# Moving VectorE's sums of x, its scaling, and the convolution kernel's products within the last pair of head groups

## The reference

```
base  = x @ W.T                                    # W 512 x 512
low   = x @ lora_A[label of b]                     # 5 labels, 512 x 32 each
x     = x + base + (low @ lora_B.T) * 0.5
K     = 2 * Re(sum_n Ct[h,n] * exp(dtA[h,n] * t))  # a kernel of 512 taps for each head
y     = causal convolution of x with K per head + x * D
x     = x + y * (position < length of b)
```

## Time and profile before

| quantity | value |
| --- | --- |
| median of 3 runs | 191.71 us (191.71 to 192.05) |
| profiled execution | 192.15 us |
| its span, first to last instruction | 190.4 us |
| TensorE busy | 185.3 us, 97% |
| VectorE busy | 141.7 us, 74% |
| ScalarE busy | 94.4 us, 50% |
| GpSimd busy | 68.1 us, 36% |

### The profile page before, as it was taken

The page is one execution under the profiler, slowest core; times in us unless marked ns, Lnnn a source line. Parts: engine busy times, 40 slices in busy tenths (PEclk is TensorE's granted clock), DMA queues, the critical chain, the costliest instruction groups (busy, mean ns, idle before and its releaser), DMA issues.

```text
span 190.4 us, 2677 instructions
## 1 busy us (share of the span) xinstructions
PE 185.3 (97%) x920; PEld 155.3 (82%) x920; DVE 141.7 (74%) x193; ACT 94.4 (50%) x149; POOL 68.1 (36%) x111
## 2 busy tenths in 40 slices
PE   7999999999999999999899999999999999999994
PEld 3487887888887888887688878889999999999994
DVE  0579979977998968778997865467777777777743
ACT  2447066098183972331663571606565656565600
POOL 6000878000000058810001034315676767676700
PEclk9999999999999999999999999999999999999999
DMA  6697997000000000000000155015887888888534
GB/s 176 155 380 281 427 422 332 4 2 0 3 2 0 0 2 0 3 0 0 0 0 9 36 193 160 5 55 121 288 284 275 281 274 276 278 284 273 190 120 156
DMA packets 14813, 27.35 MB, mean 144 GB/s; under 512 B 2608, under 2 KB 5072, under 8 KB 13904
## 3 DMA queue, kind: packets, MB, share of 16 engines
q1 hardware_dynamic: 14128, 26.66, 40.9%
q10 hardware_dynamic: 672, 0.52, 1.0%
HBM read 18.71 MB, written 8.47 MB: 143 GB/s over the span
## 4 chain that ended last, share of the span: by engine, by line
PE 77%; DVE 9%; POOL 6%; ACT 4%; issue 3%; DVEq 0%; POOLq 0%
PE k_ps L810 13%; PE k_ps L792 6%; POOL tmp L420 5%; PE k_ps L793 5%; PE k_ps L794 5%; PE y_ps L725 5%; PE y_ps L726 5%; PE y_ps L727 5%; DVE low_sel L1043 5%; PE k_ps L811 3%; PE y_ps L741 3%; DVE phase L1063 2%; PE y_ps L745 2%; PE y_ps L732 2%; PE low_ps L719 2%
## 5 line engine op out<-in xcount | busy, mean ns | idle before, releaser
L502 POOL TENSOR_TENSOR t_lo<-w_raw,t_hi 128x512 fp32r<-128x512 f32 x32 | 40.9, 1284 | 38.4 <-ACT t_hi L571 38.4
L1115 DVE COPY_PREDICATED x_all<-len_mask,k_ps 128x512 f32<-128x512 int32 x31 | 23.4, 753 | 16.0 <-PE k_ps L794 16.0
L565 ACT CAST xs_hi<-x_all 128x512 fp32r<-128x512 f32 x32 | 19.9, 623 | 26.0 <-PE k_ps L794 26.0
L725 PE MATMUL y_ps<-x_hi,w_hi 128*128 128x512 f32 x72 | 28.2, 392 | 0.0
L726 PE MATMUL y_ps<-x_hi,w_lo 128*128 128x512 f32 x72 | 28.1, 390 | 0.0
L727 PE MATMUL y_ps<-x_lo,w_hi 128*128 128x512 f32 x72 | 28.1, 390 | 0.0
L1043 DVE COPY_PREDICATED low_sel<-lab_mask,low_ps 32x512 f32<-32x512 int32 x32 | 23.4, 731 | 3.4 <-PE low_ps L855 1.1
L792 PE MATMUL k_ps<-xs_hi,t_hi 128*128 128x384 f32 (+1 forms) x68 | 22.3, 327 | 0.0
L1055 DVE TENSOR_TENSOR xs_lo<-x_all,xs_hi 128x512 fp32r<-128x512 f32 x32 | 22.0, 692 | 0.0
L793 PE MATMUL k_ps<-xs_hi,t_lo 128*128 128x384 f32 (+1 forms) x68 | 20.8, 306 | 0.0
L794 PE MATMUL k_ps<-xs_lo,t_hi 128*128 128x384 f32 (+1 forms) x68 | 20.8, 305 | 0.0
(11 more groups left out here) (216 smaller groups left out, 403.6 us busy)
## 6 DMA issues: line engine op xcount, KB each, us to landing
w_raw<-k_pad SPq DMA_DIRECT2D x32, 256.0 KB, 4.2
out<-x_all SPq DMA_DIRECT2D x31, 256.0 KB, 3.4
x_all<-in_xt SPq DMA_DIRECT2D x7, 1024.0 KB, 12.0
w_raw<-in_wt SPq DMA_DIRECT2D x3, 256.0 KB, 4.5
x_all<-in_xt SPq DMA_DIRECT2D x3, 256.0 KB, 4.7
a_raw<-in_a_lab SPq DMA_DIRECT2D x1, 320.0 KB, 5.5
w_raw<-in_wt ACTq DMA_DIRECT2D x1, 256.0 KB, 3.2
x_all<-in_xt ACTq DMA_DIRECT2D x1, 256.0 KB, 4.3
```

Of the source, the lines that this page charges most:

```text
L502: g.tensor_tensor(t_lo[:, k % TR, :], t_raw[:, k % RAW, ::-1], f32(t_hi[:, k % TR, :]), ALU.subtract).then_inc(t_lo_done, 1)
L565: s.copy(xs_hi[:, h % XR, :], x_all[:, h, :]).then_inc(xs_hi_done, 1)
L725: mm(o, w_hi[:, c, cols(d)], moving(x_hi, g, c), start=(c == 0), stop=False, skip_group_check=True)
L1115: v.copy_predicated(x_all[:, h, :], mask, y2_ps[h % 2]).then_inc(o_done, 1)
```

## The change

VectorE makes all four sums of x, and the low parts of T3 and T2, in group 4's step; `k_scale` moves from group 4's step behind group 5's selection, where it stands ahead of `k_factors_lo`. ScalarE casts T2 ahead of `stack_low(5)` instead of behind it, and `copy_k` moves from between `evict(5, 2)` and `evict(5, 3)` to behind `stack_low(6)`. TensorE does `k_matmuls` behind the pair's products of A instead of ahead of group 5's last `times_b`, and M6 ahead of M1, which keeps the wait for `k_copied`. Branches that `PAIRS = (6,)` never takes are removed.

```diff
-        m_order = ("M1", "M6", "M5", "M7", "M2", "M3", "M4")
+        m_order = ("M6", "M1", "M5", "M7", "M2", "M3", "M4")
...
                 if g == FIRST - 1:
                     split_op_hi(0, "T3")
+                    split_op_hi(0, "T2")
                 if g != 1:
                     stack_low(g)
-                if g == FIRST - 1:
-                    split_op_hi(0, "T2")
...
                     split_op_hi(0, "T4")
                     split_op_hi(0, "T1")
-                    copy_k()
                 evict(g, 3)
...
                 stack_low(g)
+                copy_k()
...
-                if g == PE_KGEN:
-                    k_matmuls()
                 times_b(g, 3)
...
                 low_of(g + 1, False, True, a_hi[:, 0:2, :], a_lo[:, 0:2, :], i, "T3").then_inc(low_done, 1)
-                if g == PE_KGEN + 1:
-                    pe.wait_ge(k_copied, 1)
...
-                for d in range(2):
-                    product(alpha, d, w11_hi, w11_lo, i, "X11", True).then_inc(m_done, 1)
+                k_matmuls()
                 wait_op(i, "T2")
...
                     product(beta, d, s_high[1], s_low[1], i, "T2", True).then_inc(m_done, 1)
+                pe.wait_ge(k_copied, 1)
+                for d in range(2):
+                    product(alpha, d, w11_hi, w11_lo, i, "X11", True).then_inc(m_done, 1)
...
                 if g == DVE_KGEN + 1:
-                    sum_x(0, "T1")
-                    sum_x(0, "T3")
-                    k_scale()
-                if g == FIRST - 1:
-                    sum_x(0, "T2")
-                    sum_x(0, "T4")
+                    for name in sum_order:
+                        sum_x(0, name)
                     split_op_lo(0, "T3")
                     split_op_lo(0, "T2")
+                if g == FIRST - 1:
+                    k_scale()
                     k_factors_lo()
                     length_mask()
```

More of the change, by code:

```diff
@@ L652, in _ @@
                     s.copy(s_high[3], s_raw[3]).then_inc(s_hi_done, 1)
-                if g == PE_KGEN + 1 and i > 0:
-                    copy_k()
                 stack_low(g)
+                copy_k()
                 act.wait_ge(op_lo_done, lo_at(i, "T4"))
@@ L662, in _ @@
                 stack_low(g + 1)
[L663 to L676, removed]
+                for h in range(LEAD):
+                    split_t_hi(h)
+                    if h < 2:
+                        split_xs_hi(h)
                 act.wait_ge(op_lo_done, lo_at(i, "T1"))
@@ L681, in _ @@
                         .then_inc(alpha_read, 1)
-                if i + 1 < len(PAIRS):
-                    split_op_hi(i + 1, "T2")
             for h in range(2, LEAD):
@@ L953, in _ @@
                 pair(i)
-                if PAIRS[i] == PE_KGEN - 1:
-                    pe.wait_ge(alpha_read, 4 * i + 4)
-                    k_matmuls()
             for h in range(LAST):
@@ L1209, in _ @@
                     mix(d, x_all[:, b, cols(d)], x_all[:, a, cols(2 + d)], beta, "M6")
-                if g == PE_KGEN - 1:
-                    k_scale()
                 for d in range(2):
@@ L1217, in _ @@
                     mix(d, u3, u3, gamma, "M5")
[L1218 to L1225, removed]
+                for h in range(2):
+                    split_xs_lo(h)
                 for d in range(2):
@@ L1231, in _ @@
                     mix(d, m1, m1, beta, "M4")
-                if i + 1 < len(PAIRS):
-                    split_op_lo(i + 1, "T2")
             for h in range(2, LEAD):
```

## The result

The changed kernel took 193.23 us (median of 7 runs, 192.31 to 193.37) against 192.05 for the kernel before in the same comparison: ratio 1.0047, 95% interval 1.003 to 1.0064, so 0.6 to 1.2 us slower. The forecast was a shift of +0.91. One launch of the kernel before took 299.04 us, far from its other six (191.71 to 192.47); no trace shows why.

What follows compares the result with a forecast made beforehand. TensorE, busy 97% of the span, was taken to bound the kernel through its waits; 0.18 from VectorE's chain and 0.73 from ScalarE's copies, +0.91 on 191.71, gave 192.6 us, range 192.3 to 193.1 (8-in-10: 191.9 to 193.3).

Steps and rivals of the forecast that it cites:

- The wait for T3's cast: VectorE before group 5's selection: T3's low part waits for ScalarE's cast, so the selection starts only 0.34 us earlier.
- the sum: Shift of group 7's `plus_b`, +0.91 us, put on the median 191.71 to give 192.6 us.
- the forecast's own range: Range of the main forecast without rivals: 192.3 to 193.1 us, chance 0.79.
- the wider one: The 8-in-10 range, taking in Rival 1 and the spread of the runs: 191.9 to 193.3 us.
- VectorE's chain: VectorE's serial work up to group 6's selection, which starts late: 0.18 us of the shift.
- ScalarE's copies: ScalarE's two copies between M1 and `stack_low(7)` hold that cast back: 0.73 us of the shift.
- a stall before M1: TensorE waits before M1 for `copy_k`, which stands behind `stack_low(6)`: about 0.8 us.
- one near 1 us at `plus_b`: TensorE, half of M5 done, waits nearly 1 us before group 7's `plus_b`.
- Rival 1: M1's copies don't hold `stack_low(7)`; `plus_b` only 0.18 late, 191.9 us, no measurable change; chance 0.09.
- Rival 2: Group 5's selection really comes early, so the kernel is faster, at the extreme 191.1 us; chance 0.07.
- rivals 3 and 4: 3: K's path delays the convolution, 193.5 and above, chance 0.04; 4: late gains delay `k_scale`, 193.0 with 0.4, chance 0.01.
- the bound of 4.5: GpSimd's last gains steps, stretched by VectorE's added sums: at most 4.5 us more, `k_gains` at 86.3.

Runs made afterwards that it cites:

- The first two runs: Changed kernel with `copy_k` ahead of `stack_low(6)`: ratio 1.0003 to the kernel before; changed kernel with `stack_low(7)` ahead of M1's copies: 1.0007.
- the mask run: Changed kernel with `length_mask` moved between `k_scale` and `k_factors_lo`, into VectorE's wait for `fac_hi`: ratio 0.9985 to the kernel before.
- The second run: Changed kernel with `stack_low(7)` ahead of ScalarE's copies of M1, `copy_k` still behind `stack_low(6)`: ratio 1.0007 to the kernel before.
- The last run: Changed kernel with `length_mask` and T2's low part in the wait for `fac_hi`, `stack_low(7)` ahead of M1's copies: 190.60 us against 191.94, ratio 0.9928.

## Why the prediction was right

**Step by step, counted from the sums.** Group 5's selection: forecast 9.05, measured 9.00. The wait for T3's cast stands in front of it, as said. `k_scale` starts at 13.49 (forecast 13.53); the idle time behind it is 1.55 (forecast 1.6). Group 6's selection: 25.25 (forecast 25.33), before 25.15. M1: 30.68 (30.82). `plus_b`: 35.76 (35.88), a shift of 0.79 where the sum gave 0.91. No term that the sum uses is off by more than 0.15. M6, put at 104.68 − 77.35 = 27.33 at the latest, began at 27.00, and the sum doesn't hang on it, since `copy_k` sets M1. The profiled span came out at 191.6 instead of 191.3 because this execution's early part was 0.43 longer.

**The median.** It came out at 193.23, 0.6 above the forecast 192.6 and just outside the forecast's own range (192.3 to 193.1), inside the wider one. Some 0.3 of that is the base: the kernel before took 192.05 in the comparison, and I had put the shift on 191.71. So the traces bear out the shift more closely than the median does.

**The two parts of the shift.** I split it into 0.18 from VectorE's chain and 0.73 from ScalarE's copies. The first two runs measure what is left without the second part: 0.14 and 0.11. So ScalarE's part is 0.65 to 0.68. The two aren't independent, as the mask run shows: with VectorE earlier, ScalarE's order still holds `stack_low(7)`, but `plus_b` is at 34.68, no later than in the kernel before. At group 6's selection VectorE's part is 0.10, where I had 0.18.

**TensorE's new stall.** The prediction told of a stall before M1 and one near 1 us at `plus_b`. Both are there, the second as 0.83 beyond the 0.23 of a step (112.48 to 113.54). The second run shows that the first costs nothing by its own length: with ScalarE's copies out of the way, TensorE only waits earlier instead of later.

**Rivals.** Rival 1 (only VectorE's chain counts) would have needed M1 by 107.4; it was released by `copy_k`, after 0.75 of idle time. Rival 2 would have needed group 5's selection 0.9 earlier; it came as forecast. The last run has it 1.1 earlier, as one of three edits, and `plus_b` gains. For rivals 3 and 4 GpSimd's timeline, which answers to the earlier trace rows:

```profile
80.57 1.25 POOL L420 TENSOR_TENSOR tmp<-tmp 128x32 f32<-128x32 f32 x1
81.91 1.21 POOL L417 TENSOR_SCALAR recip<-recip 128x32 f32<-128x32 f32 x1
...
83.93 0.25 POOL L420 TENSOR_TENSOR tmp<-tmp,recip 128x32 f32<-128x32 f32 x1
...
118.13 4.22 POOL L502 TENSOR_TENSOR t_lo<-w_raw,t_hi 128x512 fp32r<-128x512 f32 x3 [9.38 <-ACT t_hi L571]
```

GpSimd's slow steps reach as far as VectorE's sums (to 83.1), and the gains end at 84.18, 7 us before `k_scale`. From the sums that is 2.0 later than before, inside the bound of 4.5. The first low window starts at 118.13, and head 0 at 127.94 never waits for it.

**One sentence was too narrow.** I wrote that VectorE and GpSimd block each other on one side only. In the changed kernel the low parts of heads 0 and 1 fall on GpSimd's second and third windows:

```profile
120.25 2.65 DVE L1030 TENSOR_TENSOR xs_lo<-x_all,xs_hi 128x512 fp32r<-128x512 f32 x2
...
121.14 1.76 DVE L1030 TENSOR_TENSOR xs_lo<-x_all,xs_hi 128x512 fp32r<-128x512 f32 x1
```

The second took 1.76, where the median of the 32 is 0.69: VectorE was held as well, as the rule of the Trainium skill cited in the prediction has it ("SBUF — State Buffer", section "Who interferes with whom"). It cost nothing, since nobody waited for that low part yet.

## What to carry to other kernels

Where engines run in program order, a moved step takes its waits along: ask what stands behind it on its own engine, and place a copy that waits for a late producer behind the work that is ready. Moving work out of one gap on an engine isn't a gain until the gap that it opens elsewhere, here the wait for `fac_hi`, is filled with something independent. And of two stalls in a row on the engine that sets the end, the first costs by its own length only what the second doesn't take up: 0.77 before M1 cost nothing where TensorE would have waited at `plus_b` anyway, 3.50 moved `plus_b` by 4.76, the slower clock included. Ask also what waits on other engines for the work behind the first stall, here ScalarE's copies.

## What the runs showed of the hardware that I had not expected

TensorE's clock: in the profiled execution of the run with M1 ahead of M6, an idle time of 3.50 us before M1 was followed by 13 steps of 0.427 us at a granted 0.50, about 2.9 us lost with the first step, almost as much again as the stall itself. One of the six executions of that kernel kept a mean clock of 1.000. Idle times of 0.75 to 1.08 us in the other runs left the steps behind the first one at 0.23.

VectorE and GpSimd: a 32-wide GpSimd step took 0.25 us beside an idle VectorE and 1.21 to 1.25 beside the sums, a single-input step (L417) as much as one with two inputs; VectorE's 128x512 subtraction took 1.76 instead of 0.69 beside GpSimd's windows.
